# Stages behind the attention in tiles of 32 tokens of all batch rows, with the attention spread evenly over an LSTM's steps, in a one-core kernel

## The chip, the cores and the metric

The kernel runs on one core of a Trainium2 chip. The metric is the device time of one execution in microseconds, the median of the runs. The engines are PE (TensorE: matrix products and transposes), DVE (VectorE), ACT (ScalarE), POOL (GpSimd) and SP, which here only issues transfers. Each runs its own list of instructions in order and waits on semaphores for the others.

## What is computed

x is 4 x 512 x 256, fp32. First a transformer block in hyperbolic space is added to x, then an LSTM over the 512 tokens is added to that. `plin` is `expmap0(logmap0(x) @ w + b)`; the maps and mobius_add only need a row's norms and dot products as factors.

```python
q, k, v = _to_heads(plin(xm, w_q, b_q)), ...          # 16 heads of 16 columns
scores = einsum('bhqd,bhkd->bhqk', qt, kt) / sqrt(HD)
out_h = expmap0(einsum('bhqk,bhkd->bhqd', softmax(scores), vt))
x = mobius_add(residual, expmap0(g_msa * logmap0(plin(_from_heads(out_h), w_o, b_o))))
xm = expmap0(layer_norm(logmap0(x)) * (1 + sc_mlp) + sh_mlp)
ff = plin(plin(xm, w_f1, b_f1), w_f2, b_f2)           # 256 -> 1024 -> 256
block = mobius_add(x, expmap0(g_mlp * logmap0(ff)))
x = x_in + block
a = x[:, t] @ Wx + b + prev_h @ Wh                    # 512 steps, each needs the one before
i, f, o, g = sigmoid(a0), sigmoid(a1), sigmoid(a2), tanh(a3)
next_c = f * prev_c + i * g;  next_h = o * tanh(next_c)
return x + h
```

## The kernel before

The work comes in four stretches. **Setup** loads weights, gets the first layer norm's factors on POOL, and splits `Wh` into two fp16 words. The **loop over 16 tiles** of 128 tokens makes q, k and v, their heads' clips, and the split, transposed k (`norm_x`, L541 on PE; L1101 to L1139 on DVE; L805 to L813 on ACT; L401 to L406 on POOL). **Block 0**, the first 128 tokens of all four batch rows, then goes through attention and all stages behind it with no step beside it. After that come the **512 steps** of the LSTM in four blocks of 128. While block j - 1 is stepped through, `whole(j, step)` puts the attention and later stages of block j between the steps, in a run-time loop over j; the last block's steps have nothing beside them.

The order is written by hand. `along_attention` walks over 68 steps: behind each step every engine does its share of one head (`scores` L578 and `weighted` L591 on PE, `exps` L830 with two exponentials of 512 columns on ACT, `low_weights` L330 with 512 columns on DVE). Then `Slots` places the later stages between the remaining 60 steps: projection (L625), squares (L871, L873) and factors (`mobius` on POOL, ended by L432), sum and statistics (L1214, L1218), logarithm and norm (`to_norm`), the feed-forward per tile in six slots (L650, L646, L660), the second mobius_add and the gates' inputs from `Wx` (L682, copied by L937).

A step (`pe_step`, `act_step`, `dve_step`) is 32 products of 8 columns (L708) into banks for A, F and O; three sums on DVE (L1239, L1241, L1243), three tanh on ACT (L944 to L948), L1246 and a scan L1249 on DVE, tanh on ACT (L950), and then h in two fp16 words (L1257, L1258, L1260), on which the next step's products wait:

```python
d.tensor_tensor(hi, by_k(oU), by_k(tC), ALU.mult).then_inc(s["l_hi"], 1)
d.tensor_tensor(h32[:], oU[:], tC[:], ALU.mult).then_inc(s["l_h32"], 1)
v.wait_ge(s["l_h32"], m)
d.tensor_tensor(lo, by_k(h32), hi, ALU.subtract).then_inc(s["l_lo"], 1)
```

Behind it stand two copies nothing urgent waits for (L1261, L1263), then DVE's share of the other work. Every 16 steps `put_round` (L691) puts the gates' inputs into the banks. POOL makes its factors by chains of operations on 1 to 4 columns, each waiting for the one before (`power` is L226).

## Time and profile before

| | us |
|---|---|
| median of 3 runs | 1853.12 (1852.63 to 1854.8) |
| the profiled execution | 1852.16 |
| its span | 1850.4 |
| PE busy | 1204.1 (65%) |
| DVE busy | 1187.2 (64%) |
| ACT busy | 929.5 (50%) |
| POOL busy | 254.4 (14%) |
| mean granted TensorE clock | 0.627 |

No engine is busy all the time. The steps depend on one another, so that an engine's busy time matters only where its other work delays a step. PEclk is the share of full speed that TensorE was granted, 0.5 being 1.2 GHz and 1.0 being 2.4 GHz. PE counts an fp32 product as two instructions.

### The profile page before, as it was taken

Reading aid. Unit: us, or ns where it says so; the run is one execution under the profiler, and the core shown is the slowest. Engines: PE = TensorE matmul, PEld = TensorE weight load, DVE = VectorE, ACT = ScalarE, POOL = GpSimd, SP = SyncE. Lnnn points to the kernel's source line nnn. Section 1 sums busy time; section 2 is a strip of 40 time slices with the busy share of each in tenths; the row PEclk is TensorE's granted clock in tenths of the full one; section 3 lists DMA queues with packets and bytes.
Section 4 is the critical chain, followed back from the end, with each engine's and each line's share of the span. In section 5 each row is a group of like instructions: output and inputs, shape, how many; then the busy total and the mean of one; then the engine's idle time right before and its main releaser. Section 6 shows DMA issues by size and latency. Waiting matters only on the chain.

```text
span 1850.4 us, 59130 instructions
## 1 busy us (share of the span) xinstructions
PE 1204.1 (65%) x21615; PEld 988.4 (53%) x21615; DVE 1187.2 (64%) x6784; ACT 929.5 (50%) x3253; POOL 254.4 (14%) x674
## 2 busy tenths in 40 slices
PE   4666577186777648867776497777754885544444
PEld 4544455155666546666665366666653674444444
DVE  6466666222888766658887566588875755666665
ACT  0333378244777545547775455577753553333333
POOL 4222200522000031300001312000023220000000
PEclk9667655588555558965555598655555985555555
DMA  8000000000000000000000000000000000000000
GB/s 264 0 0 0 0 1 1 1 1 1 3 3 3 2 2 2 2 27 3 3 3 2 2 2 2 27 3 3 3 2 2 2 2 13 2 2 2 2 2 13
DMA packets 14654, 19.17 MB, mean 10 GB/s; under 512 B 3348, under 2 KB 13208, under 8 KB 14360
## 3 DMA queue, kind: packets, MB, share of 16 engines
q1 hardware_dynamic: 10248, 10.50, 1.8%
q10 hardware_dynamic: 4112, 4.86, 0.9%
q8 instruction: 172, 2.82, 0.6%
q14 instruction: 122, 1.00, 0.2%
HBM read 13.25 MB, written 2.10 MB: 8 GB/s over the span
## 4 chain that ended last, share of the span: by engine, by line
PE 42%; DVE 25%; ACT 12%; issue 11%; POOL 7%; DMA 1%; POOLq 1%; ACTq 1%; DVEq 0%; SPq 0%
PE psum L708 21%; DVE cnew L1249 4%; ACT tC L950 4%; DVE h L1257 3%; DVE h L1260 3%; PE psum L682 3%; DVE gO L1243 3%; PE psum L691 3%; POOL sc L226 3%; PE psum L650 3%; PE psum L660 2%; PE psum L541 2%; DVE cadd L1246 2%; DVE h L1258 2%; PE psum L578 2%
## 5 line engine op out<-in xcount | busy, mean ns | idle before, releaser
L708 PE MATMUL psum<-h,wh 128*128 128x8 f16 x16384 | 514.5, 168 | 419.5 <-DVE h L1260 402.5
L708 PEld LDWEIGHTS psum<-h,wh 128*128 128x128 f16 x16384 | 477.8, 103 | 533.2 <-DVE h L1260 501.8
L944 ACT ACTIVATE tA<-gA 128x16 f32<-128x16 f32 x512 | 110.5, 216 | 475.3 <-DVE gA L1239 475.1
L1239 DVE TENSOR_REDUCE gA<-psum 128x16 f32<-128x32 f32 x512 | 97.3, 190 | 180.1 <-PE psum L708 179.7
L578 PE MATMUL psum<-qT,kT 64*128 64x128 f16 x1024 | 153.8, 303 | 12.7 <-ACT weights L830 11.4
L950 ACT ACTIVATE tC<-cnew 128x8 f32<-128x8 f32 x512 | 108.8, 213 | 90.1 <-DVE cnew L1249 37.0
L830 ACT ACTIVATE weights<-psum 128x512 f16<-128x512 f32 x256 | 153.0, 598 | 0.0
L1257 DVE TENSOR_TENSOR h<-oU,tC 128x8 f16<-128x8 f32 x512 | 89.1, 174 | 94.7 <-ACT tC L950 94.1
L1249 DVE TENSOR_TENSOR_SCAN cnew<-cmul,cadd 128x24 f32<-128x24 f32 x512 | 107.7, 210 | 29.1 <-DVE cadd L1246 1.5
L1246 DVE SCALAR_TENSOR_TENSOR cadd<-tA 128x8 f32<-128x8 f32 x512 | 84.3, 165 | 52.4 <-ACT tA L944 44.6
L946 ACT ACTIVATE cmul<-gF 128x8 f32<-128x8 f32 x512 | 107.5, 210 | 0.0
L948 ACT ACTIVATE tO<-gO 128x8 f32<-128x8 f32 x512 | 105.6, 206 | 0.3
L591 PE MATMUL psum<-vs,weights 128*128 128x33 f16 x2048 | 101.7, 192 | 1.1 <-DVE weights L330 1.1
L578 PEld LDWEIGHTS psum<-qT,kT 64*128 64x128 f16 x1024 | 86.7, 127 | 26.0 <-ACT weights L830 11.4
L1260 DVE TENSOR_TENSOR h<-h 128x8 f16<-128x8 f32 x512 | 88.5, 173 | 18.1
L1243 DVE TENSOR_REDUCE gO<-psum 128x8 f32<-128x16 f32 x512 | 88.4, 173 | 16.1
L445 POOL TENSOR_SCALAR sc<-sc 128x64 f32<-128x64 f32 x4 | 1.9, 465 | 695.1 <-ACT sc L855 695.1
L330 DVE TENSOR_TENSOR weights<-tmp,weights 128x512 f16<-128x512 f32 x128 | 87.6, 684 | 13.7 <-ACT weights L830 13.7
L330 DVE TENSOR_TENSOR weights<-fT,weights 128x512 f16<-128x512 f32 x128 | 87.6, 684 | 11.3 <-ACT weights L830 11.3
L1241 DVE TENSOR_REDUCE gF<-psum 128x8 f32<-128x16 f32 x512 | 88.4, 173 | 8.4
L591 PEld LDWEIGHTS psum<-vs,weights 128*128 128x128 f16 x2048 | 80.3, 107 | 13.4 <-issue 10.6
L830 ACT ACTIVATE fT<-psum 128x512 f32<-128x512 f32 x128 | 76.2, 595 | 22.3 <-PE psum L591 21.8
(222 smaller groups left out, 2196.8 us busy)
## 6 DMA issues: line engine op xcount, KB each, us to landing
arena<-in_x_dram SPq DMA_DIRECT2D x4, 512.0 KB, 9.7
wf<-in_L_cond_w_f_dram SPq DMA_DIRECT2D x2, 1024.0 KB, 19.8
xs<-in_x_dram SPq DMA_DIRECT2D x4, 512.0 KB, 5.4
out_dram<-place SPq DMA_DIRECT2D x16, 128.0 KB, 1.7
arena<-in_L_cond_w_ada_dram ACTq DMA_DIRECT2D x1, 1536.0 KB
weights<-in_L_cond_Wh_dram ACTq DMA_DIRECT2D x1, 1024.0 KB, 14.3
gates<-in_L_cond_b_ada_dram ACTq DMA_DIRECT2D x8, 128.0 KB, 15.3
wx<-in_L_cond_Wx_dram SPq DMA_DIRECT2D x1, 1024.0 KB, 22.3
```

What stands on the lines that cost most here:

```text
L330: return engine.tensor_tensor(weights[:, buf, 1, kcs, :], w32[buf][:, half], weights[:, buf, 0, kcs, :], ALU.subtract)
L578: last = mm(bank[half][:, kc * P:(kc + 1) * P], tile_of(kT, b)[rows, hp, kc * P:(kc + 1) * P], qT[rows, hp, :], start=True, stop=True, ski ...
L591: last = mm(sums(h), weights[:, hp % 2, wl, 2 * e + kc // 2, kc % 2 * P:(kc % 2 + 1) * P], tile_of(vs, b)[:, kc, h, :], start=kc == 0 and ...
L708: last = mm(cols, wh16[:, half, kc, (g0 + g) * P:(g0 + g + 1) * P], h16[:, kc, :, :], start=False, stop=g == n - 1 and kc == KD - 1 and ha ...
L830: last = A(dst.rearrange("p a b -> p (a b)"), bank[half], ACT.Exp, scale=1.0 / (math.sqrt(HD) * QK_UP * QK_UP))
L944: A(tA[:], gA[:], ACT.Tanh, scale=down).then_inc(s["l_tA"], 1)
L950: A(tC[:], cnew[:, :, 2], ACT.Tanh, scale=0.5).then_inc(s["l_tC"], 1)
L1243: d.tensor_reduce(gO[:], gate_cols(pO, 2, r), axis=AX.X, op=ALU.add).then_inc(s["l_gO"], 1)
L1246: d.scalar_tensor_tensor(cadd[:, :, 2], tA[:, 0:8], 1.0, tA[:, 8:16], ALU.add, ALU.mult).then_inc(s["l_ig"], 1)
L1249: d.tensor_tensor_scan(cnew[:].rearrange("p c e -> p (c e)"), cmul[:].rearrange("p c e -> p (c e)"), cadd[:].rearrange("p c e -> p (c e)") ...
L1257: d.tensor_tensor(hi, by_k(oU), by_k(tC), ALU.mult).then_inc(s["l_hi"], 1)
L1260: d.tensor_tensor(lo, by_k(h32), hi, ALU.subtract).then_inc(s["l_lo"], 1)
```

## The change

- **The names.** A *slot* `t` runs from -192 to 511 on every engine (`for t in range(FIRST, T)`). From slot 0 on, each slot begins with recurrence step `t`; behind it `pieces` places the slot's share of the attention, of `merged` (the 16 heads of one tile brought together), of `post` (all stages behind the attention) and of the output. Nothing is a loop at run time any more: all 704 slots are written out, on every engine.
- **Attention.** One head takes two slots instead of one: its scores and its first exponential (fp32) in the even slot, its second exponential (fp16) in the odd one, its low words on DVE in two halves of 256 columns, its product with the values five slots after its scores. 96 of the 256 heads come before step 0, the other 160 ride along with steps 0 to 319.
- **Tiles behind the attention.** A tile is 32 tokens of each of the 4 batch rows (128 rows), so that one tile feeds 32 steps; before, it was 128 tokens of one batch row, and four of them fed 128 steps. `post(n, r)` runs tile n through r = 0 to 47, from slot 32n - 48; two tiles overlap in each 16 slots. Tile 0 is done wholly before step 0, and tile 1 to r = 15. `merged(k, r)` stands 32 slots apart, r = 0 to 8.
- **Transposed q.** q is split and transposed in the loop over the 16 tiles (`qstack`, `p_hq`, `p_qT`) and copied by ACT to `qTs`, behind the copy of k; before, this was done tile by tile in the attention (`q_twice`, `q_transposed`, `q_columns`).
- **Factors.** mobius_add's factors, the clips and the norm's factor are made on POOL for one tile (width 1) instead of four or two. The logarithm is no longer ACT's `Ln`: it is an estimate from the float's bits (DVE copy, POOL scale) with one correction by `Exp`, so that the table of functions is never changed in the slots. The gates' rows are multiplied by DVE instead of POOL (L437).
- **Feed-forward.** The first product is made transposed (16 products of 128 columns with `wf1` as the stationary side), ACT adds the bias column while copying, so that the 8 transposes and both DVE passes over 512 columns go; the norm of the hidden row is now the product of the squares `fsq` with a column of ones, 8 products with one column each.
- **Step.** The low half of h comes from a scan over 24 columns that multiplies and subtracts at once, in place of the product h32 and a subtraction; h for the output is a product of its own, behind it. `put_round`, the fp32 products that put 16 steps' gates into PSUM, stands ahead of its step instead of right behind the step before.
- **Transfers.** x comes in and the output leaves in pieces of 32 rows, four DMAs a tile, 16 tiles.

The core of the diff, with the pieces that the prediction speaks of:

```diff
+FIRST = -192
+PAUSE = 48
+HEADS = B * NB * H
+RING = 32
 ROUND = 16
...
+def head_slot(n):
+    return FIRST + 2 * n
...
+def merged_slot(k):
+    return head_slot(H * k + H - 1) + 6
...
+def pieces(g, attention, merged, post, out):
+    attention(g)
+    k = (g - merged_slot(0)) // RING
+    if 0 <= k < NT:
+        merged(k, g - merged_slot(k))
+    newest = (g + PAUSE) // RING
+    for n in (newest - 1, newest):
+        if 0 <= n < NT and g + PAUSE - RING * n < PAUSE:
+            post(n, g + PAUSE - RING * n)
+    if g > RING and g % RING == 1:
+        out(g // RING - 1)
...
+            def post(n, r):
...
+                if r == 1:
+                    hold(pool, "n_n1", n + 1)
+                    hold(pool, "n_n2", n + 1)
+                    mobius_arg(ch, "A", "n_ar")
+                if r == 4:
+                    hold(pool, "n_xa", n + 1)
+                    hold(pool, "n_xq", n + 1)
+                    hold(pool, "n_th", n + 1)
+                    mobius_factors(ch, "A", one("xq"), "n_ab")
+                if r == 8:
+                    hold(pool, "n_st", n + 1)
+                    to_ratio(ch, 1, mv1[:, 0:1], mv1[:, 1:2], one("x2q"), s["n_z"])
+                if r == 10:
...
+                if r == 12:
...
+                    to_norm(ch, 1, mv1[:, 0:1], mv1[:, 1:2], one("kapn"), one("negm"), s["n_km"], km_out_scaled=False)
+                if r == 21:
+                    hold(pool, "n_nu", n + 1)
+                    clip(ch, one("sun"), one("nun"), 1, one("cau"), one("cbu"), s["n_su"])
+                if r == 31:
+                    hold(pool, "n_nfc", n + 1)
+                    clip(ch, one("sfn"), one("nfn"), 1, one("caf"), one("cbf"), s["n_sf"])
+                if r == 34:
+                    hold(pool, "n_n3", n + 1)
+                    mobius_arg(ch, "B", "n_ar2")
+                if r == 37:
+                    hold(pool, "n_xa2", n + 1)
+                    hold(pool, "n_th2", n + 1)
+                    mobius_factors(ch, "B", one("x2q"), "n_ab2")
...
+            for t in range(FIRST, T):
+                pieces(t, lambda t: None, merged, post, lambda n: None)
...
+            def attention(t):
+                if t % 2 == 1 and 0 <= (t - 5 - FIRST) // 2 < HEADS:
+                    weighted((t - 5 - FIRST) // 2)
+                if t % 2 == 0 and (t - FIRST) // 2 < HEADS:
+                    scores((t - FIRST) // 2)
...
+                if 25 <= r < 29:
+                    i = r - 25
+                    pe.wait_ge(s["n_uc"], n + 1)
+                    if i > 0:
+                        pe.wait_ge(s["n_fc"], 4 * n + i)
+                    for c in (2 * i, 2 * i + 1):
+                        for kc in range(KD):
+                            last = mm(pP[:, c % 4 * P:(c % 4 + 1) * P], wf1[:, kc, c * P:(c + 1) * P], uT[:, 0, kc, :],
+                                      start=kc == 0, stop=kc == KD - 1, skip_group_check=True)
+                    last.then_inc(s["n_f"], 1)
+                if 29 <= r < 33:
+                    i = r - 29
+                    if i == 0:
+                        pe.wait_ge(s["n_fc"], 4 * n + 4)
+                    for kc in (2 * i, 2 * i + 1):
+                        last = mm(pP[:, 0:D], fT[:, kc, :], wf2[:, kc, :], start=kc == 0, stop=kc == KF - 1, skip_group_check=True)
+                    if i == 3:
+                        last.then_inc(s["n_f2"], 1)
+                if r in (30, 31):
+                    if r == 30:
...
+                    for c in range(4 * (r - 30), 4 * (r - 30) + 4):
+                        last = mm(pM[:, 0:1], fsq[:, c, :], ones[:, 0:1], start=c == 0, stop=c == KF - 1, skip_group_check=True)
+                    if r == 31:
+                        last.then_inc(s["n_nf"], 1)
...
+                if 42 <= r < 46:
+                    i = r - 42
...
+                    for gi in (2 * i, 2 * i + 1):
+                        c = CHUNK[gi]
+                        for kc in range(KD):
+                            last = mm(pP[:, gi % 4 * P:(gi % 4 + 1) * P], wx[:, kc, c * P:(c + 1) * P], XT[:, kc, :],
+                                      start=kc == 0, stop=kc == KD - 1, skip_group_check=True)
+                    last.then_inc(s["n_g"], 1)
...
+            def low_weights(m, half):
+                part = slice(half * T // 2, (half + 1) * T // 2)
+                v.wait_ge(s["t_e"], m + 1)
+                d.tensor_tensor(weights[:, m % 2, 1, part], w32[:, m % 2, part], weights[:, m % 2, 0, part], ALU.subtract).then_inc(s["t_l"], 1)
...
-                hi, lo = (h16[:, :, :, half] for half in range(2))
-                by_k = lambda t: t[:].rearrange("p (k b) -> p k b", b=B)
-                d.tensor_tensor(hi, by_k(oU), by_k(tC), ALU.mult).then_inc(s["l_hi"], 1)
-                d.tensor_tensor(h32[:], oU[:], tC[:], ALU.mult).then_inc(s["l_h32"], 1)
-                v.wait_ge(s["l_h32"], m)
-                d.tensor_tensor(lo, by_k(h32), hi, ALU.subtract).then_inc(s["l_lo"], 1)
+                by_k = lambda t: t.rearrange("p (k b) -> p k b", b=B)
+                d.tensor_tensor(hcol, by_k(oU), by_k(tC), ALU.mult).then_inc(s["l_hi"], 1)
+                v.wait_ge(s["l_hi"], m)
+                d.tensor_tensor_scan(lo3, ot3[:].rearrange("p c e -> p (c e)"), hi3, 0.0, ALU.mult, ALU.subtract).then_inc(s["l_lo"], 1)
```

How the order moves, on PE where the feed-forward stands between the steps. `wf`, `fT` and `arena` are the feed-forward's weights and hidden rows (`arena` holds `fT` and `fsq` in the changed kernel), `h` and `hl` are the LSTM's state. Before, in a row:

```order
L708 MATMUL psum<-h,wh 128x8 x32
L643 REGISTER_ALU
L646 MATMUL psum<-ident,tmp 128x128 x4
L650 MATMUL psum<-wf,uT 128x512
L702 REGISTER_ALU
L708 MATMUL psum<-h,wh 128x8 x32
L660 MATMUL psum<-wf,fT 128x256 x3
L631 MATMUL psum<-ident,xn 128x128 x2
L702 REGISTER_ALU
L708 MATMUL psum<-h,wh 128x8 x32
L646 MATMUL psum<-ident,tmp 128x128 x4
L660 MATMUL psum<-wf,fT 128x256
```

After, from the slot with r = 30 on, into the slot with r = 32, which is also r = 0 of the next tile:

```order
L562 MATMUL psum<-qTs,kT 128x128 x4
L634 MATMUL psum<-wf,arena 128x256 x2
L647 MATMUL psum<-ones,arena 128x1 x4
L687 MATMUL psum<-hl,wh 128x8 x32
L574 MATMUL psum<-vs,weights 128x33 x8
L634 MATMUL psum<-wf,arena 128x256 x2
L647 MATMUL psum<-ones,arena 128x1 x4
L677 MATMUL psum<-arena,ident 128x256
L677 MATMUL psum<-arena,ident 128x128 x2
L687 MATMUL psum<-hl,wh 128x8 x32
L562 MATMUL psum<-qTs,kT 128x128 x4
L634 MATMUL psum<-wf,arena 128x256 x2
```

Each step's 32 products are followed by a head's scores (L562) or its product with the values (L574), and then by the products behind the attention, and in front of every sixteenth step stand the three of L677.

On DVE, behind the last small operation of a step, where a tile's statistics are made. Before:

```order
L1214 SCALAR_TENSOR_TENSOR place<-place,sc 128x256
L1218 BN_STATS mv<-place 128x6
L1220 BN_AGGR mv<-mv 128x2
L1238 REGISTER_ALU
L1239 TENSOR_REDUCE gA<-psum 128x16
```

After, at the slot where r = 40 of one tile meets r = 8 of the next (`X` is the rows of the residual, `weights` the attention's low words):

```order
L1032 TENSOR_TENSOR weights<-w,weights 128x256
L1123 SCALAR_TENSOR_TENSOR X<-X,sc,xr 128x256
L1125 SCALAR_TENSOR_TENSOR X<-place,sc,X 128x256
L1093 BN_STATS mv<-X 128x6
L1095 BN_AGGR mv<-mv 128x2
L1131 TENSOR_REDUCE gA<-psum 128x16
```

Three long operations more stand between a step's end and the next step's sum L1131: half a head's low words, and the two of the older tile's second mobius_add.

## Rows read from the trace of the kernel before

**Rows 1.** Stretches: length, busy us and count of each engine, PEclk, DMA share, GB/s.
```profile
242.00:324.60 82.60, 63.35 (x808) 44.55 (x808) 52.91 (x106) 74.13 (x142) 0.00 (x0) 0.51 0.01 1
324.60:452.90 128.30, 67.44 (x318) 48.35 (x319) 25.75 (x66) 47.72 (x128) 46.19 (x133) 0.78 0.00 1
452.90:816.60 363.70, 262.04 (x5266) 217.73 (x5265) 257.29 (x1583) 212.12 (x779) 45.87 (x133) 0.63 0.02 4
1539.30:1850.40 311.10, 144.38 (x4146) 132.06 (x4146) 193.72 (x1412) 106.19 (x512) 0.00 (x0) 0.50 0.02 5
```

**Rows 2.** Timeline of one plain step, last block: start, us, engine, line, operation.
```profile
1560.92 1.02 PE L708 MATMUL psum<-h,wh 128*128 128x8 f16 x32 [1.34 <-DVE h L1260]
1561.55 0.19 DVE L1239 TENSOR_REDUCE gA<-psum 128x16 f32<-128x32 f32 x1 [0.53 <-PE psum L708]
...
1562.77 0.17 DVE L1257 TENSOR_TENSOR h<-oU,tC 128x8 f16<-128x8 f32 x1 [0.17 <-ACT tC L950]
...
1563.05 0.17 DVE L1260 TENSOR_TENSOR h<-h 128x8 f16<-128x8 f32 x1
...
1563.28 1.01 PE L708 MATMUL psum<-h,wh 128*128 128x8 f16 x32 [1.34 <-DVE h L1260]
```

**Rows 3.** Timeline of a step that carries attention.
```profile
1304.86 0.68 DVE L330 TENSOR_TENSOR weights<-fT,weights 128x512 f16<-128x512 f32 x1
...
1305.72 0.39 PE L591 MATMUL psum<-vs,weights 128*128 128x33 f16 x8
...
1306.04 0.60 PE L578 MATMUL psum<-qT,kT 64*128 64x128 f16 x4
...
1307.52 0.60 ACT L830 ACTIVATE weights<-psum 128x512 f16<-128x512 f32 x1
```

**Rows 4.** The chain of waits where one block ends and the next begins.
```profile
812.23 4.60 issue
```

**Rows 5.** Timeline of the loop over 16 tiles: POOL, DVE, ACT.
```profile
132.22 0.57 POOL L226 TENSOR_TENSOR sc<-sc,cst 128x1 f32<-128x1 f32 x1 [0.18 <-POOL sc L274]
...
133.44 0.73 DVE L1132 CAST qhl<-place 128x256 f32 x1 [0.21 <-DVE place L1124]
134.10 0.28 DVE L1133 CAST words<-place 128x256 f16<-128x256 f32 x1
...
137.29 1.02 ACT L813 ACTIVATE kT<-psum 128x1024 f16 x1 [6.53 <-PE psum L560]
```

**Rows 6.** POOL in its chains: a power 16 columns wide; a product 4 wide.
```profile
22.13 2.94 POOL sc L226
...
347.45 0.20 POOL L432 TENSOR_TENSOR sc<-sc 128x4 f32<-128x4 f32 x1 [0.18 <-POOL sc L431]
```

**Rows 7.** Timeline, DVE work between two steps, behind the attention.
```profile
669.79 0.48 DVE L1214 SCALAR_TENSOR_TENSOR place<-place,sc 128x256 f32<-128x256 f32 x1
670.30 0.43 DVE L1218 BATCH_NORM_STATS2 mv<-place 128x6 f32<-128x256 f32 x1
670.88 0.18 DVE L1220 BATCH_NORM_AGGREGATE mv<-mv 128x2 f32<-128x6 f32 x1 [0.15 <-DVE mv L1218]
```

**Rows 8.** Timeline of TensorE: fp32 products at either clock.
```profile
699.54 0.99 PE L639 MATMUL psum<-ones,usq 128*128 128x1 f32 x4
...
708.91 1.14 PE L691 MATMUL psum<-arena,ident 128*128 x6
709.89 1.46 PE L660 MATMUL psum<-wf,fT 128*128 128x256 f32 x6
...
769.68 3.54 PE L682 MATMUL psum<-uT,wx 128*128 128x128 f32 x16
...
778.27 2.05 PE L682 MATMUL psum<-uT,wx 128*128 128x128 f32 x16 [1.07 <-ACT uT L928]
```

**Rows 9.** A stretch of feed-forward work between steps; columns as in rows 1.
```profile
710.00:750.00 40.00, 37.70 (x617) 28.40 (x615) 29.05 (x185) 23.43 (x97) 10.42 (x31) 1.00 0.01 2
```

**Rows 10.** Timeline of ACT: four copies of the gates' inputs.
```profile
773.38 1.63 ACT L937 ACTIVATE arena<-psum,blc,unit 128x128 f32 x4 [0.96 <-PE psum L682]
```

More of the change, by code:

```diff
@@ L752, in _ @@
[L752 to L762 removed]
+                last.then_inc(s["t_AV"], 1)
+            def attention(t):
[3 more added lines that the diff above has]
+                    scores((t - FIRST) // 2)
@@ new lines, in gate_products @@
+            def gate_products(which, r):
+                bk, g0, w = GATE_BANKS[which]
+                for c in range(w):
+                    cols = gate_cols(which, r)[:, c * B:(c + 1) * B, :]
+                    for kc in range(KD):
+                        for half in range(2):
+                            last = mm(cols, wh16[:, half, kc, (g0 + c) * P:(g0 + c + 1) * P], hl[:, :, kc, :, 2].rearrange("p e b -> p b e"),
+                                      start=False, stop=c == w - 1 and kc == KD - 1 and half == 1, skip_group_check=True)
+                return last
@@ L764, in _ @@
+            for t in range(FIRST, T):
+                if t >= 0:
+                    step(t)
+                pieces(t, attention, merged, post, out_rows)
+            out_rows(NT - 1)
         @block.scalar
@@ L801, in _ @@
             act.sem_inc(s["p_kc"], 1)
+            act.sem_inc(s["p_qc"], 1)
             norm_x(0, 0, True)
@@ L943, in act_step, with step @@
+            def step(i):
+                m = i + 1
                 act.wait_ge(s["l_gA"], m)
@@ L1012, in _ @@
-            whole(0, None)
-            down = nc.scalar.alloc_register("down")
-            nc.scalar.reg_load(down, big1[0:1, 0:1].bitcast(I32))
-            with act.Fori(1, NB) as j:
-                whole(j, act_step)
-            for i in range(P):
-                act_step((NB - 1) * P + 1 + i, None, i % ROUND)
+                A(tC, cnew[:, :, 2], ACT.Tanh, scale=0.5).then_inc(s["l_tC"], 1)
+            for t in range(FIRST, T):
+                if t >= 0:
+                    step(t)
+                pieces(t, attention, merged, post, lambda n: None)
@@ L1341 @@
+            for t in range(FIRST, T):
+                if t == 0:
+                    v.wait_ge(s["n_xc"], 4)
+                    v.wait_ge(s["h0_s"], 1)
+                    d.tensor_tensor(xw[:, 0], xw[:, 0], h0c[:], ALU.add).then_inc(s["l_x0"], 1)
+                if t >= 0:
+                    step(t)
+                pieces(t, attention, merged, post, out_rows)
+            out_rows(NT - 1)
 _INS = ["x", "cond_1024"] + [f"L0_cond_{n}" for n in ("w_q", "b_q", "w_k", "b_k", "w_v", "b_v", "w_o", "b_o", "w_f1", "b_f1",
```

1104 lines of the change are left out of this document (437 added, 667 removed).

## The prediction

> **What bounds the kernel now.** I read the stretches first, then single steps in the timeline, then the chain of waits at one boundary. The stretches [rows 1] give four parts: up to 242.0 us setup and the loop over 16 tiles; to 324.6 the attention of block 0, where ACT is busy 74.13 of 82.6 us; to 452.9 the later stages of block 0, where no engine is busy for more than half and the chain between engines sets the time; then the 512 steps. The last block has nothing beside its steps: 311.1 us, of which some 5.7 lie behind its last step, so a plain step takes 2.36 us [rows 2], 2.355 over the block. Inside it PE is busy 1.02 us and idle 1.34, and DVE has about 0.68 us between its last small copy and the next sum L1239, which starts 0.63 us after PE. The first 384 steps take 1539.3 - 452.9 = 1086.4 us, 182 more than 384 plain steps (904). With the last block's 4 that is **186 us that other work adds to the steps**. The attention itself adds next to nothing: the step of [rows 3] has one head's two exponentials on ACT (0.60 each), 0.68 us of DVE and 0.39 + 0.60 us of PE, and it is as long as a plain one. So the price of work between steps is what overflows an engine's gap, and of the 186 us most stands in the 60 steps a block that carry the later stages. Some is neither: at a block's end the chain shows 4.60 us of "issue" [rows 4], in which PE waits for nothing but its instructions.
>
> **The change, up to step 0.** The loop over tiles gets a second ACT copy of 1024 columns behind that of k. The one of k takes 1.02 us [rows 5] and ACT's square of the next tile waits behind it, so each of 16 rounds grows by up to 1.02 us. DVE's cast of q took 0.73 us where the cast of k took 0.28 [rows 5]. If the run-time address is what made it slow, the written-out target gives back 0.45. If it is POOL, which works in the same moment, nothing comes back. I take 0.8 a round from the two ends 0.57 and 1.02: **+13 us** (9 to 16), so 255, and 256 at the first exponential.
> The Trainium skill (SBUF — State Buffer, "SBUF: two separate sides") says that VectorE and GpSimd share one pair of ports, which one of them holds for a whole instruction. By that rule the loop would pay the 16 us.
>
> Then 72 of the 96 heads run alone, at two exponentials or 1.2 us a head [rows 1, 3]: 86 us. In them four tiles are merged. DVE waits at r = 7 for POOL's chain that began at r = 2: some 12 operations of 0.20 + 0.18 us idle [rows 6], and a power 16 columns wide, 2.94 us [rows 6], in all 8 us, where five slots of 0.6 us give 3. ACT runs one slot ahead and loses 4 us, and 0.8 for its two extra copies: 4 x 5 = 20 us. That is 362. Tile 0 now goes alone from r = 0 to 47: POOL's chains (two of 7, two of 13, one of 10, one of 29 operations and two clips, 10 of them powers at 0.57 + 0.18 [rows 5]) are 39 us; PE, ACT and DVE in between, by their rows, 40 us. Tile 1's first 16 slots push two of POOL's chains in front of tile 0's, +10, and 24 heads share the slots, +8: 97 us. Block 0's four tiles took 128.3 us for the same [rows 1]. **Step 0 starts at 459 us instead of 452.9: +6.** Ends: 435 (all waits for POOL hidden) to 485.
>
> **The step.** Today L1257 starts at 1562.77 and L1260 at 1563.05, and PE 0.23 later [rows 2]. The new low half waits for the high half's end (0.17 + 0.04) and is a scan of 24 columns, which in this kernel (L1249) takes 0.04 more than L1260. 0.21 + 0.04 against 0.28: 0.025 us less a step, **-13 us** over 512. Ends: 0 and -20.
>
> **Other work between the steps.** An excess is what an engine's share adds beyond its gap. With attention, the gaps left are about 0.7 (even slots) or 0.9 us (odd) on PE, 0.35 on DVE (half a head's low words take some 0.33 of 0.68) and 0.9 on ACT; without it 1.34, 0.68 and 1.4. One tile's 32 slots, with attention:
> - DVE: an operation of 256 columns is 0.48 [rows 7], a dependent second one 0.05 later. r = 20 (two, and a sum of heads in the same slot): 1.0. r = 33 with the next tile's r = 1 (three): 1.1. r = 40 with r = 8 (two, then statistics, 0.43 and 0.18 with 0.15 idle [rows 7]): 1.3. Three single ones: 0.4.
> - POOL: r = 4 of the new tile stands in front of r = 37 of the old one on its queue. 13 operations take 5.5 us each, so DVE at r = 40 is 1.1 us early: 1.1.
> - PE with ACT, feed-forward one (r = 24 to 28): each slot 4 fp32 products of 128 columns, 8 of which took 3.54 us at 1.2 GHz and 2.05 at 2.4 [rows 8]. Two slots still at 1.2 GHz: 0.85 and 1.05. Then two at 2.4 where ACT ends last, one with the squares, one with the merged tile's copy: 0.9 and 0.85. Transposes: 0.1.
> - PE, feed-forward two (r = 29 to 32): 256 columns at 0.5 us a product, one column at 0.25, half of the 0.99 for two at 1.2 GHz [rows 8]. r = 29: 0.15. r = 30, scores 0.6 + 1.0 + 1.1: 1.4. r = 31: 1.2. r = 32 with r = 0 and `put_round` (1.14 [rows 8]): 2.9. The period's other `put_round`: 0.8.
> - Gates (r = 42 to 45): 4 products, then two ACT copies of 0.4 us [rows 10]: 1.2, 0.6, 0.4, 0.2.
>
> Sum 17.5 us. 10 tiles lie beside attention: 175. Five lie beside steps alone; with the wider gaps the same list gives, in its order, 0.3, 0.8 and 1.0 on DVE, 1.1 for POOL, 1.2 and 3.9 for the two feed-forwards, 0.4 for the other `put_round`, 1.2 for the gates: 9.9, or 50 in all. The last period: 1. **226 us instead of 186: +40.** It replaces the block boundaries [rows 4] and ACT's table changes, which 186 contains and 226 doesn't. Everything is written out; the last block was too and ran at 2.355, so that costs nothing. Row transfers lie on SP, three tiles ahead: nothing. Behind the last step one tile instead of four: **-1**.
>
> Here the clock is weighed. Attention alone ran at 0.51 and plain steps at 0.50 [rows 1], but the dense feed-forward of block 1 at 1.00 with PE busy 37.70 of 40 us [rows 9]. The spread work is nearly gapless on PE from r = 25 to 32 and again at r = 42, so I take two slots at 1.2 GHz in each and 2.4 behind them.
> The Trainium skill (TensorE: Matmul & The Clock Gate, The HAM clock gate) says that the slow clock is the default and sustained activity lifts it. By that rule work spread thinly pays the slow price; it is the third rival.
>
> The sum: +6 - 13 + 40 - 1 = +32 on the profiled execution's 1852.2 us, which lies 1 us under the median: **1884 us**.
>
> **Rivals.** (1) *The clock stays up*, so the spread work fits. If PE keeps 2.4 GHz through r = 24 to 47, the slots at 1.2 GHz lose 2.9 us a tile and the scores 1.0: 10 x 3.9 + 5 x 2.0 = 49, **1835 us**, faster. It decides from 32 us on, or 2.1 a tile. For it: 1.00 in [rows 9], in which the steps' own narrow products were a third of PE's time. Against: the attention slots, busier than plain ones, ran at 0.51. (2) *The waits for POOL are hidden*: step 0 at 435 (-24) and no wait at r = 40 (-17): **1843 us**. For it: ACT and PE have slack there. Against: each engine's order is fixed. (3) *The clock never rises*: the same products at the slow prices of [rows 8] add 9.0 us a tile with attention and 7.5 without: +127, **2011 us**. For it: rows 1's 0.63 mean and the gaps of r = 33 to 41. Against: [rows 9].
>
> **How the numbers follow.** The forecast has 0.45, rival 1 0.27, rival 2 0.13, rival 3 0.15. The forecast's own range is 1860 to 1930, from the ends of the start and 3 us a tile. The whole range, 1815 to 1960, takes in rivals 1 and 2 and leaves out most of 3. A difference under 0.2% (3.7 us) can't be told from none here. Faster: rivals 1 and 2 nearly whole, 0.38; same 0.05; slower 0.57.
>
> **What would show it.** First product of a step at 459 us. 2.33 us for a plain step. Periods of 32 steps some 92 us long beside attention and 85 without. PEclk above 0.9 only in r = 27 to 33. Waits of DVE on POOL at r = 40. The prediction is wrong if periods beside attention take under 88 us, or if the clock is at one level throughout.

## The result: 5% slower, and the profile after

The changed kernel takes **1955.4 us** (median of 4 runs, 1936.2 to 1981.3) against 1853.0 for the one before: ratio 1.051, 95% interval 1.046 to 1.057. The forecast was 1884, so slower was right and the size was not: +102 us instead of +32. The profiled execution took 1959.4 us, of which 1957.6 are its span. The run of 1981.3 us counts as slow, because it lies over 1.5% above the fastest, and is left out of the ratio; four later runs of the same kernel, none of them slow, took 1949 to 1972 us.

The four runs alone already say where to look. They took 1936.2, 1951.3, 1959.4 and 1981.3 us, at a mean granted clock of 0.569, 0.560, 0.555 and 0.542, while the kernel before repeats within 2.2 us, at 0.627 in its profile. From the page of the changed kernel: the span, the busy times, TensorE's share and clock in the 40 slices.

```profile
span 1957.6 us, 60062 instructions
PE 1378.3 (70%) x22071; PEld 1183.1 (60%) x22071; DVE 1170.0 (60%) x6481; ACT 914.1 (47%) x3335; POOL 553.8 (28%) x1726
PE   3665666556787878787878787878776757675764
PEclk9767655565656555555555555555555555555555
```

From the 12th slice on the granted clock stands near 0.5 (a digit 5 is 0.50 to 0.59), that is at 1.2 GHz nearly throughout. The stretches, in the columns of [rows 1]: attention alone, tile 0 on its own, ten periods of 32 steps beside attention.

```profile
255.90:365.90 110.00, 67.81 (x852) 47.13 (x852) 60.62 (x170) 75.05 (x152) 27.73 (x52) 0.50 0.01 1
365.90:462.26 96.36, 48.70 (x405) 37.71 (x405) 26.92 (x82) 39.13 (x97) 42.19 (x141) 0.59 0.01 2
462.26:1422.85 960.59, 755.63 (x13411) 658.73 (x13409) 634.41 (x3767) 515.94 (x1994) 308.72 (x1002) 0.53 0.02 5
```

TensorE's products other than the steps' own, in the view of groups by line and shape: total busy time and the mean of one instruction in ns (an fp32 product is two instructions).

```profile
L663 PE MATMUL psum<-place,wx 128*128 128x128 f32 x512 | 130.4, 436 | 6.9 <-ACT arena L870 6.4
L626 PE MATMUL psum<-uT,wf 128*128 128x128 f32 x512 | 127.5, 429 | 1.1 <-ACT arena L845 0.8 <-ACT uT L838 0.2
L634 PE MATMUL psum<-wf,arena 128*128 128x256 f32 x256 | 114.6, 593 | 0.5 <-ACT arena L845 0.5
L647 PE MATMUL psum<-ones,arena 128*128 128x1 f32 x256 | 47.2, 305 | 0.0
```

The same work in the kernel before:

```profile
L682 PE MATMUL psum<-uT,wx 128*128 128x128 f32 x512 | 76.0, 312 | 10.7 <-ACT uT L928 10.7
L650 PE MATMUL psum<-wf,uT 128*128 128x512 f32 x128 | 74.9, 698 | 0.0
L660 PE MATMUL psum<-wf,fT 128*128 128x256 f32 x256 | 65.7, 389 | 1.0 <-ACT fT L910 1.0
```

The first three groups went from 217 us to 373 us with no more arithmetic in them: before, they came in dense stretches that ran mostly at 2.4 GHz; now they mostly run at 1.2. The eight one-column products a tile, which sum the squares of the feed-forward's hidden layer, came with the change (L647, 256 instructions; before, L639 had 64 for another norm).

**A tile whose clock rises and one whose clock does not.** The order of instructions is the same in all periods beside attention, and yet they are 89.8 to 99.0 us long. In order of time: 90.9, 89.8, 96.0, 93.7, 99.0, 98.6, 98.5, 98.9, 98.6, 94.4; then without attention 92.5, 92.3, 92.2, 92.3, 87.4; then the last, 73.1. I call g the step's number within its period; r = g + 16 for the tile in its later stages. Three slots make 7.0 of the 8.8 us between the second and the seventh period, g = 14, 15 and 16 (r = 30 to 32): feed-forward two, the norm's products, `put_round`, the next tile's output projection. The rest is in g = 12 and 13 (1.05 and 0.65 us). Here they are on TensorE in the second period, from the timeline:

```profile
591.48 0.95 PE L647 MATMUL psum<-ones,arena 128*128 128x1 f32 x8
592.29 1.00 PE L687 MATMUL psum<-hl,wh 128*128 128x8 f16 x32
593.14 0.35 PE L574 MATMUL psum<-vs,weights 128*128 128x33 f16 x8
593.35 1.11 PE L634 MATMUL psum<-wf,arena 128*128 128x256 f32 x4
594.29 0.95 PE L647 MATMUL psum<-ones,arena 128*128 128x1 f32 x8
595.10 1.12 PE L677 MATMUL psum<-arena,ident 128*128 128x256 f32 x6
596.06 1.00 PE L687 MATMUL psum<-hl,wh 128*128 128x8 f16 x32
```

And in the seventh:

```profile
1071.54 1.71 PE L647 MATMUL psum<-ones,arena 128*128 128x1 f32 x8
1073.11 1.00 PE L687 MATMUL psum<-hl,wh 128*128 128x8 f16 x32
1073.96 0.39 PE L574 MATMUL psum<-vs,weights 128*128 128x33 f16 x8
1074.19 2.05 PE L634 MATMUL psum<-wf,arena 128*128 128x256 f32 x4
1076.03 1.71 PE L647 MATMUL psum<-ones,arena 128*128 128x1 f32 x8
1077.60 2.05 PE L677 MATMUL psum<-arena,ident 128*128 128x256 f32 x6
1079.45 1.05 PE L687 MATMUL psum<-hl,wh 128*128 128x8 f16 x32
```

In these rows TensorE has no gap in either period, so its work is the slot. Only the fp32 products change price: 0.95 or 1.71, 1.11 or 2.05, 1.12 or 2.05. The steps' own 32 narrow products take 1.00 to 1.05 us either way. The slots g = 14 to 16 are 3.16, 3.65 and 3.81 us long in the second period, and 4.90, 6.39 and 6.34 in the seventh. The stretches around these rows and the two whole periods:

```profile
555.22:645.00 89.78, 69.21 (x1338) 60.89 (x1338) 63.33 (x376) 51.41 (x200) 30.63 (x100) 0.61 0.02 5
1032.39:1130.94 98.55, 78.45 (x1338) 68.08 (x1338) 63.32 (x376) 51.52 (x200) 30.59 (x100) 0.50 0.02 5
...
590.80:601.40 10.60, 10.29 (x156) 8.96 (x155) 5.92 (x37) 4.34 (x17) 1.02 (x3) 1.00 0.01 2
1052.50:1086.70 34.20, 34.20 (x410) 29.74 (x407) 15.71 (x95) 14.43 (x54) 3.72 (x12) 0.50 0.01 2
```

The counts are equal (1338, 376, 200, 100). What differs is the clock of one stretch. In the seventh period TensorE is busy without a gap for 34.2 us and stays at 1.2 GHz. [Rows 9], from which I took that dense work has 2.4 GHz, did not carry over. Beside attention, the clock of a period rises in g = 11 to 13 or late in g = 16, and in no period of this profile in g = 14 or 15. Five of the ten (the fifth to the ninth) never get it. The third has it from g = 11 and loses it in g = 14, before most of the crowded work; the fourth and the tenth lose it in g = 15 and get it back for the end of g = 16.

**The wait at r = 40**, in VectorE's timeline:

```profile
1107.38 0.48 DVE L1123 SCALAR_TENSOR_TENSOR X<-X,sc,xr 128x256 f32<-128x256 f32 x1 [1.56 <-POOL sc L430]
```

VectorE stands 1.56 us, and the sums of the next step stand behind it. Over the run the view of waits has this one at 26.2 us in 15 times, the longest 4.2 us.

### The profile page after: what moved, and what is told of

Same layout as the page of the kernel before. It is cut to its first block, busy times and chain, and to the rows that moved or that the text cites. A ratio compares the mean times of both kernels' runs of the same rounds, so it can differ in the third digit from the quotient of the medians.

```text
span 1957.6 us, 60062 instructions
## 1 busy us (share of the span) xinstructions
PE 1378.3 (70%) x22071; PEld 1183.1 (60%) x22071; DVE 1170.0 (60%) x6481; ACT 914.1 (47%) x3335; POOL 553.8 (28%) x1726
## 3 DMA queue, kind: packets, MB, share of 16 engines
q10 hardware_dynamic: 3392, 3.81, 0.7%
## 4 chain that ended last, share of the span: by engine, by line
PE 46%; DVE 13%; POOL 11%; issue 8%; ACT 8%; POOLq 1%; DVEq 0%; ACTq 0%
PE psum L687 18%; PE psum L663 7%; PE psum L626 6%; PE psum L634 5%; POOL sc L231 4%; PE psum L677 3%; DVE cnew L1140 3%; ACT ot L885 2%; DVE hl L1149 2%; PE psum L647 2%; DVE hl L1147 2%; PE psum L562 2%; DVE gO L1135 2%; ACT w L783 1%; ACT weights L787 1%
## 5 line engine op out<-in xcount | busy, mean ns | idle before, releaser
L687 PE MATMUL psum<-hl,wh 128*128 128x8 f16 x16384 | 525.9, 172 | 347.0 <-DVE hl L1149 346.4
L687 PEld LDWEIGHTS psum<-hl,wh 128*128 128x128 f16 x16384 | 505.9, 104 | 427.8 <-DVE hl L1149 408.0
L1131 DVE TENSOR_REDUCE gA<-psum 128x16 f32<-128x32 f32 x512 | 96.8, 189 | 281.4 <-PE psum L687 276.6
L1032 DVE TENSOR_TENSOR weights<-w,weights 128x256 f16<-128x256 f32 x512 | 208.2, 419 | 39.8 <-ACT weights L787 38.8
L231 POOL TENSOR_TENSOR sc<-sc,cst 128x1 f32<-128x1 f32 (+1 forms) x260 | 201.1, 773 | 48.1 <-POOL sc L279 18.1
L562 PE MATMUL psum<-qTs,kT 64*128 64x128 f16 x1024 | 151.1, 299 | 6.4 <-ACT weights L787 4.5
L783 ACT ACTIVATE w<-psum 128x512 f32<-128x512 f32 x256 | 149.8, 585 | 7.9 <-DVE weights L1032 5.5
L663 PE MATMUL psum<-place,wx 128*128 128x128 f32 x512 | 130.4, 436 | 6.9 <-ACT arena L870 6.4
L574 PE MATMUL psum<-vs,weights 128*128 128x33 f16 x2048 | 100.9, 191 | 39.8 <-DVE weights L1032 22.9
L626 PE MATMUL psum<-uT,wf 128*128 128x128 f32 x512 | 127.5, 429 | 1.1 <-ACT arena L845 0.8
L663 PEld LDWEIGHTS psum<-place,wx 128*128 128x128 f32 x512 | 112.9, 325 | 13.8 <-issue 11.6
L574 PEld LDWEIGHTS psum<-vs,weights 128*128 128x128 f16 x2048 | 78.8, 106 | 61.4 <-DVE weights L1032 56.9
L634 PE MATMUL psum<-wf,arena 128*128 128x256 f32 x256 | 114.6, 593 | 0.5 <-ACT arena L845 0.5
L626 PEld LDWEIGHTS psum<-uT,wf 128*128 128x128 f32 x512 | 112.4, 323 | 3.9 <-issue 3.1
## 6 DMA issues: line engine op xcount, KB each, us to landing
oT<-in_L_cond_Wh_dram ACTq DMA_DIRECT2D x1, 1024.0 KB, 14.4
```

The source lines that it names most:

```text
L231: ch.link(nc.gpsimd.tensor_tensor(dst, src, cst[:, which, 0:w], ALU.pow))
L562: last = mm(bank[m % 2][:, kc * P:(kc + 1) * P], kT[part, b, hp, kc * P:(kc + 1) * P], qTs[part, k, hp, :], start=True, stop=True, skip_gr ...
L574: last = mm(pV[:, h % 8 * W1:(h % 8 + 1) * W1], weights[:, m % 2, wl, kc * P:(kc + 1) * P], vs[:, k % B, kc, h, :], start=kc == 0 and wl = ...
L626: last = mm(pP[:, c % 4 * P:(c % 4 + 1) * P], wf1[:, kc, c * P:(c + 1) * P], uT[:, 0, kc, :], start=kc == 0, stop=kc == KD - 1, skip_group ...
L634: last = mm(pP[:, 0:D], fT[:, kc, :], wf2[:, kc, :], start=kc == 0, stop=kc == KF - 1, skip_group_check=True)
L663: last = mm(pP[:, gi % 4 * P:(gi % 4 + 1) * P], wx[:, kc, c * P:(c + 1) * P], XT[:, kc, :], start=kc == 0, stop=kc == KD - 1, skip_group_c ...
```

## The experiments

Two questions. Is the crowded stretch paid for by TensorE's work at whatever clock it has (**crowded slots**), or does something in the changed instruction stream (narrow products instead of 512-column ones, one-column products, gaps) hold the clock down (**clock rivals**)? And is the wait for POOL worth its length?

**Width of the products.** The changed kernel with one product of 512 columns for the four of 128 in each feed-forward slot. It leaves out the sum over the two halves of the inputs.

```diff
-for c in (2 * i, 2 * i + 1):
-    for kc in range(KD):
-        last = mm(pP[:, c % 4 * P:(c % 4 + 1) * P], wf1[:, kc, c * P:(c + 1) * P], uT[:, 0, kc, :], ...)
+last = mm(pP[:, :], uT[:, 0, i % 2, :], wf1[:, i % 2, i // 2 * 512:(i // 2 + 1) * 512], ...)
```

> Leaves out the feed-forward's first product as it should be: in place of 4 fp32 products of 128 columns a slot (r = 25 to 28) stands one of 512 columns, the same number of columns, without the sum over both halves, so that its output is not the reference's. Everything behind it stays. Theory A (what keeps TensorE at 1.2 GHz in the changed kernel is that its dense slots are made of products of 128 and 8 columns): the granted clock rises to 1.00 from about r = 27 on in most periods, the slots r = 30 to 32, now 4.9, 6.4 and 6.35 us, fall to about 3.0, 3.8 and 3.8, and the whole falls by 10 x 9 + 5 x 4 us to about 1850. Theory B (the work is simply too much for one kernel's slots at any mix, the clock follows the short gaps before and behind): the clock stays at 0.50, r = 25 to 28 get 0.3 us shorter each at most, the whole stays above 1930.

Measured: 1962.7 us, clock 0.555: nothing came of it. The other way round, the kernel before with its wide products cut into pieces of 128 columns. Its text below says that the sums are the same. They are not, and the output is not the reference's; but TensorE gets the same columns, in four or two times as many products.

> The kernel before with each feed-forward product of 512 columns cut into four of 128 and each of 256 into two of 128; nothing else changes, the sums are the same. Theory A: the stretch 710 to 750 us no longer has a granted clock of 1.00 but mostly 0.50, and the three blocks get longer, each by 10 to 20 us, the whole at 1885 to 1910. Theory B: the clock stays near 1.00 there and the whole rises by at most 10 us for the extra weight loads.

Measured: 1858.2 us, ratio 1.003 (1.002 to 1.005), clock 0.625. Its dense stretch, with the columns of [rows 9]:

```profile
705.00:750.00 45.00, 42.79 (x772) 40.95 (x771) 31.91 (x201) 25.78 (x105) 9.05 (x27) 0.97 0.01 3
```

Cut products ran at 2.4 GHz in the kernel before, and with the first product widened the changed one stayed at its low clock. The width of the feed-forward's products is not the cause.

**Gaps between the steps.** Extra products behind each of the 14 light slots a period (g = 0 to 7, 19 to 24); nothing is left out. First two or three fp16 ones of 256 columns:

```diff
+if 0 <= t < 480 and t % RING in (0, 1, 2, 3, 4, 5, 6, 7, 19, 20, 21, 22, 23, 24):
+    for _ in range(2 if t % 2 == 0 else 3):
+        mm(pP[:, 0:256], ident16[:], wh16[:, 0, 0, 0:256], ...)
```

> The changed kernel with idle gaps of PE filled: in the slots r = 35 to 40 and r = 48 to 55 of a period (of 32) two (even) or three (odd) fp16 products of 256 columns into a bank nobody reads then. If columns streamed are what is missing in the light slots (theory A in its strong form), the clock is at 1.00 when the feed-forward begins, r = 25 to 32 shrink by 10 us a period, and the whole falls to about 1830 to 1850. If not, the clock stays at 0.50 and the light slots grow by 0 to 0.2 us each, the whole stays within 1940 to 1990.

Measured: 1960.0 us, clock 0.552. Then two fp32 ones of 128 columns in the same places (`mm(pP[:, 0:128], ident[:], wx[:, 0, 0:128], ...)`):

> The changed kernel with two extra fp32 products of 128 columns (onto a free PSUM bank) behind each of the light slots g = 0 to 7 and 19 to 24; nothing is left out. A slot has some 1 us in which TensorE is idle, and two such products take 0.9 us at 1.2 GHz by the row of L663 (439 ns per instruction, two a product), so the light slots should stay within 0.3 us of 2.33 us. Theory (idle gaps between the steps are what keeps the clock low, whichever type fills them): the granted clock of the light slots and of g = 9 to 17 rises, mean clock above 0.65, and the time falls toward 1840 to 1900 us. Rival (filling the gaps does not raise the clock, as the fp16 products did not): the clock stays at 0.55 and the time at 1955 to 2010 us, by what the fillers add to 14 slots a tile.

Measured: 1967.6 us, clock 0.553. The light slots grew by up to 0.2 us as allowed for, and the clock did not rise for it:

```profile
690.00:700.00 10.00, 10.00 (x143) 9.41 (x143) 5.73 (x36) 6.32 (x24) 0.00 (x0) 0.50 0.01 2
700.00:710.00 10.00, 10.00 (x102) 8.70 (x102) 3.99 (x24) 3.11 (x11) 0.00 (x0) 0.50 0.01 2
...
sum 200.00, PE 185.05 PEld 162.97 DVE 129.01 ACT 104.75 POOL 61.41; mean PE 9.25 PEld 8.15 DVE 6.45 ACT 5.24 POOL 3.07
```

TensorE was busy 185 of 200 us (620 to 820), at 1.2 GHz in every 10 us of them. So filling the gaps did not bring the clock there; three of its later periods had 2.4 GHz in g = 14 and 15 all the same, where the unaltered kernel had two.

**The norm's products.** Seven of the eight left out (and with them most of the norm's sum):

```diff
-for c in range(4 * (r - 30), 4 * (r - 30) + 4):
-    last = mm(pM[:, 0:1], fsq[:, c, :], ones[:, 0:1], start=c == 0, stop=c == KF - 1, ...)
+if r == 31:
+    last = mm(pM[:, 0:1], fsq[:, 0, :], ones[:, 0:1], start=True, stop=True, ...)
```

> Leaves out 7 of the 8 products that sum the squares of the hidden row (the norm comes from one eighth of the row, so that the output is not the reference's). If r = 30 and 31 are bound by PE at 1.2 GHz, each loses 3 to 4 products of 0.5 us (r = 30: 2.0 us, r = 31: 1.5 us), 3.5 us a period with 15 periods, about 50 us: 1900. If ACT, DVE or POOL ended those slots, the time would hardly change (above 1940).

Measured: 1886.4 us, 69 less, clock 0.575. The products alone explain 48 of it at the slow price (7/8 of 2 x 1.71 us in 16 tiles), and less where the clock had risen; the rest is the clock. Next a version that computes all, with the squares and the ones in bf16:

```diff
-fsq = arena[:, 3072:4096].rearrange("p (c t) -> p c t", c=KF)
+fsq = arena[:, 3072:3584].bitcast(BF16).rearrange("p (c t) -> p c t", c=KF)
...
-last = mm(pM[:, 0:1], fsq[:, c, :], ones[:, 0:1], ...)
+last = mm(pM[:, 0:1], fsq[:, c, :], ones16[:, 0:1], ...)
```

> The squares of FF1's output are written in bf16 and summed by products in bf16 instead of fp32; the eight products stay where they are and everything is computed. In the changed kernel's cold tile L647 took 16 x 0.334 us by the profile's sum of 3.4 us less overlaps, and leaving seven of the eight out gave 69 us back. Crowded slots (TensorE sets the length of the slots r = 30 and 31, at either clock): a bf16 product of one column should take what the narrow fp16 ones take, near 0.17 to 0.19 us each, so 8 x 0.43 - 8 x 0.18 = 2.0 us a tile less, 16 tiles, 32 us: about 1923 us, and slots g14 and g15 fall from 4.9 and 6.4 to near 3.9 and 5.4 us. Rival (the narrow fp32 products are what holds the clock down in the crowded stretch): the clock stands at 2.4 GHz in those slots in most tiles and the time falls to 1880 or below. Rival (products of one column are bound by their weight load whatever the type): no change, 1955.

Measured: **1888.8 us** (1876 to 1900), ratio to before 1.016 (1.013 to 1.020): 67 less, twice the forecast.

```profile
L649 PE MATMUL psum<-ones,arena 128*128 128x1 bf16 x128 | 8.6, 171 | 0.0
```

The 47.2 us of L647 became 8.6. The crowded slots of a period at 1.2 GHz (the one from 1014.4), on TensorE:

```profile
1054.80 2.06 PE L636 MATMUL psum<-wf,arena 128*128 128x256 f32 x4
1056.64 0.29 PE L649 MATMUL psum<-ones,arena 128*128 128x1 bf16 x4
1056.80 2.05 PE L679 MATMUL psum<-arena,ident 128*128 128x256 f32 x6
```

Four products take 0.29 us where they took 1.71, and slots g14 and g15 are 3.48 and 4.97 us instead of 4.90 and 6.39: 2.8 us a tile, of which I had expected 2.0. With 0.4 in g16, in which the clock now rises near the end, such a period is 95.3 us long instead of 98.5. Over sixteen tiles that is some 50 us. The rest of the 67 is the clock: of the ten periods beside attention only three are that long, and two are at 88.4 and 88.9. Slot g = 16 had its short length of 3.81 us in seven of the ten, where the changed kernel had it in two. In g = 14 and 15 the gain is not clear: three of ten against two. The clock rival doesn't hold in its clean form: were the one-column fp32 products what holds the clock down, all tiles would have the high one now. Whether the shorter stretch or the missing fp32 products brought the clock to g = 16 is not separated by this run.

**The wait for POOL.** VectorE's two instructions at r = 40, and the transposes and gate products behind them, one slot later (in the diff VectorE's block first, then that of TensorE, which ScalarE's follows).

```diff
-if r == 40:
+if r == 41:
     v.wait_ge(s["n_ab2"], n + 1)
...
-if r == 41:
+if r == 42:
...
-if 42 <= r < 46:
+if 43 <= r < 47:
```

> The two VectorE instructions of r = 40 (L1123, L1125) stand one slot later, and the transposes and gate products behind them one slot later too; nothing else changes. Theory: VectorE waited there 1.56 us for POOL's last factor (L430 of the changed kernel), and the recurrence of step 25 stood behind it; one slot later the factor is there. Expected: slot g24 falls from 5.08 to about 3.5 us, 16 tiles x 1.56 = 25 us less, about 1930 us. Rival (POOL or the gates are late next, so the wait only moves, to the first put_round behind the gates): slots g31 and g0 grow by what g24 loses, 1955 us.

Measured: **1907.8 us** (1905 to 1921), 48 less. In VectorE's timeline the instructions no longer wait:

```profile
1096.55 0.48 DVE L1123 SCALAR_TENSOR_TENSOR X<-X,sc,xr 128x256 f32<-128x256 f32 x1
1097.07 0.48 DVE L1125 SCALAR_TENSOR_TENSOR X<-place,sc,X 128x256 f32<-128x256 f32 x1
```

Slot g24 fell from 5.08 to 2.50 us, by more than the wait: the statistics of the next tile (r = 8) stand there alone now. Summed over the run, the slots g = 4, 17 and 24 lost 36 us, the gate slots and g = 31 grew by 10, and g = 13 to 16 lost 28: as in the last experiment, fewer periods were long there. Nothing in those slots was changed, so what stands elsewhere in a period bears on the clock that its crowded slots meet. All four runs (1905 to 1921) lie below all eight of the unaltered kernel (1936 to 1981).

**Both together.**

> norm16 and late40 together. They touch different slots, so their gains should add: 1955 - 32 - 25 = 1898 us. If it is far below the sum of the two, the clock has risen in more tiles; if above, one gain hid in the other.

Measured: **1846.8 us** (10 runs, 1845.6 to 1854.8), 109 less than the change and below the kernel before: ratio 0.997 (0.996 to 0.999). The measured gains add (67 + 48 = 115), but the forecast of 1898 was 51 us too high, and by its own words that means that the clock has risen in more tiles. So it has: g = 14 and 15 stood at 2.4 GHz in eight of the ten periods beside attention, g = 16 in all ten, and those periods are 86.1 to 88.9 us long. The ten runs are 9 us apart, and those of the unaltered kernel 36 us (1936 to 1972).

**One more product out of the crowded slots:** on top of both, the bias of the output projection (L611, 555 ns an instruction) as two bf16 products.

```diff
-mm(pM[:, 0:D], ones[0:1, :], bo[0:1, :], start=False, stop=True, ...).then_inc(s["n_wo"], 1)
+for half in range(2):
+    last = mm(pM[:, 0:D], ones16[0:1, :], bo16[0:1, half, :], start=False, stop=half == 1, ...)
+last.then_inc(s["n_wo"], 1)
```

> The version with the bf16 norm sums and the later second residual, and besides the output projection's bias added by two bf16 products (high and low part of the bias) in place of one fp32 product, in slot g16. In the changed kernel L611 took 2 x 0.71 us by the profile's rows, 1.2 us of TensorE at 1.2 GHz; two bf16 products of 256 columns should take some 2 x 0.25 us. Crowded slots: slot g16 falls by 0.7 us where TensorE is at 1.2 GHz there and by 0.35 us where it is at 2.4 GHz, 15 tiles, so 1847 - 5 to 10 = 1837 to 1842 us. Rival (VectorE and ScalarE end that slot): no change, 1847.

Measured: **1842.7 us** (6 runs), ratio to before 0.9945 (0.9932 to 0.9958), the fastest of all: 0.3% under the last one by the two ratios, at the upper end of the forecast.

```profile
L615 PE MATMUL psum<-bo,ones 1*128 1x256 bf16 x32 | 6.4, 281 | 0.0
```

It took 0.3 us from slot g16 (3.81 to 3.52), in which TensorE had the higher clock in all periods beside attention, here as in the version before it.

**Does the instruction stream decide?** The changed kernel a second time, unaltered:

> The changed kernel itself, unaltered, for a second profile. Theory (whether the clock rises in the crowded slots of a tile is not decided by the instruction stream): other tiles than in the first profile show the long slots g14 to g16 (4.9, 6.4, 6.3 us), periods again lie between 90 and 99 us, and time and mean clock move together as in the first four runs (1936 us at 0.569 to 1981 at 0.542). Rival (the stream decides): the same tiles, 65 to 96 and 129 to 288, are the long ones, and the profiled time is within 3 us of 1959.

Measured: 1964.3 us (1949 to 1972). Periods of the profiled execution (1972.5 us): 98.5, 98.5, 98.5, 93.7, 98.9, 98.5, 98.5, 98.8, 98.5, 94.3, 87.0, 91.9, 92.0, 92.1, 87.4. The first and second periods, which ran at 2.4 GHz in their crowded slots in the first profile, did not in this one. The eleventh did, and only in this one. The rows are those of the second and the eleventh:

```profile
564.10:662.60 98.50, 78.44 (x1338) 68.03 (x1338) 63.23 (x376) 51.51 (x200) 30.60 (x100) 0.50 0.02 5
...
1442.43:1529.38 86.95, 60.23 (x1162) 54.70 (x1162) 53.20 (x344) 36.25 (x167) 29.29 (x99) 0.56 0.02 6
```

Last, the same with 30 wide fp32 products once ahead of step 0:

```diff
+if t == 0:
+    pe.wait_ge(s["n_xc"], 4)
+    for _ in range(30):
+        mm(pP[:, 0:D], ident[:], wx[:, 0, 0:D], ...)
```

> The changed kernel with 30 extra fp32 products of 256 columns once, ahead of step 0: by the row of L634 (593 to 672 ns per instruction, two a product) some 37 us of TensorE at 1.2 GHz, or 18 if the clock rises within them. Nothing else changes. Both theories: the clock goes to 2.4 GHz somewhere in this stretch of pure wide products if density alone decides (then about 25 us); it stays at 1.2 GHz (37 us) if it does not. Behind it the same 511 steps; if the tile's place in time decides the clock of the crowded slots, other tiles than before are the long ones, and the time is 1955 + 25 to 37 with a spread of 25 us around it; if the stream decides, exactly the delay is added.

Measured: 1953.4 and 1971.4 us. Step 0 came 18 us later, and the clock rose within the products:

```profile
460.00:470.00 10.00, 9.00 (x45) 7.30 (x42) 0.95 (x3) 3.21 (x8) 5.13 (x21) 0.55 0.00 0
470.00:480.00 10.00, 10.00 (x48) 8.81 (x47) 0.00 (x0) 0.00 (x0) 2.01 (x9) 1.00 0.01 2
```

Behind them other periods were the long ones: 93.6, 98.5, 98.5, 98.5, 94.1, and then 89.7, 91.0, 89.9, 91.0, 90.5, where the unaltered kernel has 98 to 99, and 94 in the tenth. So the 18 us more left the time where it was. Whether a tile meets the high clock is not decided by its instruction stream alone: the two profiles of the unaltered kernel show it. That the shift brought the other pattern is not shown, since the pattern also changed without it. That less work in and around the crowded slots meets the high clock more often is clearest in the version with both changes: eight of its ten periods had it in g = 14 and 15, against two and one in the profiles of the unaltered kernel and five in this one. What exactly decides stays open.

## Why the prediction was right in direction and wrong in size

Its steps in order, with the other work between the steps as the excess of each slot over 2.33 us, added up over all periods of the first profile. 511 steps at 2.33 are 1190.6 us; the trace has 1488.4 from the first step's last instruction (464.35) to the last step's (1952.73), so 297.7 us of other work.

| term | predicted | measured |
|---|---|---|
| first exponential / first output projection | 256 / 362 | 255.9 / 365.9 |
| tile 0 on its own | 97 | 96.4 |
| first product of a step | 459 | 462.3 |
| plain step | 2.33 | 2.33 |
| beside attention: VectorE and POOL slots (r = 20, 33, 40) | 49 | 45.6 |
| feed-forward one (r = 25 to 28) | 37.5 | 34.3 |
| **feed-forward two, norm, `put_round` (r = 29 to 32)** | 56.5 | **87.0** |
| **gates** | 24 | **37.7** |
| other `put_round`, rest | 8 | 8.3 |
| without attention: VectorE and POOL | 16 | 13.2 |
| feed-forward one | 6 | 10.2 |
| **feed-forward two, norm, `put_round`** | 19.5 | **43.6** |
| **gates** | 6 | **14.4** |
| rest, last period | 3 | 3.4 |
| sum of the other work | 226 | 297.7 |

The spans differ by 107.2 us. Of these 9.4 are the start (+6 forecast), -12.8 the step (-13), 111.7 the other work (297.7 for 186; +40 forecast), and -1 the end (-1). So 72 of the 75 us between 1884 and the profiled 1959.4 are other work, and the four bold rows alone are 77 over; the remaining rows are 5 under.

The steps themselves, the start within 3 us, and the structure of a period were right: the scan of 24 columns took the place of the last product ([rows 2]) as costed (0.28 less 0.25 is 0.03, where the prediction writes 0.025; measured were 2.355 to 2.33), and plain steps follow each other at 2.33 us:

```profile
1931.52 0.17 DVE L1147 TENSOR_TENSOR hl<-ot 128x8 f16<-128x8 f32 x1 [0.18 <-ACT ot L885]
1931.73 0.21 DVE L1149 TENSOR_TENSOR_SCAN hl<-ot,hl 128x24 f16<-128x24 f32 x1
...
1934.06 0.21 DVE L1149 TENSOR_TENSOR_SCAN hl<-ot,hl 128x24 f16<-128x24 f32 x1
```

The start was forecast from two ends, because VectorE's slow cast of q could be due to its run-time address or to POOL. The trace decides it. The cast of q, now to a written-out place, is short. The cast of k, which starts while POOL's product runs, is now the slow one (0.28 before, [rows 5]):

```profile
137.45 0.29 DVE L1009 CAST qstack<-place 128x256 f16<-128x256 f32 x1
137.54 0.68 POOL L375 TENSOR_TENSOR osq<-place,sc 128x256 f32<-128x256 f32 x1
137.66 0.71 DVE L1010 CAST stack<-place 128x256 f16<-128x256 f32 x1
```

So the slow cast goes with POOL's work and nothing came back. The first exponential came at 255.9 us, 13.9 behind 242.0; the two ends were 9 and 16.

**The step that failed** is "so I take two slots at 1.2 GHz in each and 2.4 behind them". The crowded slots r = 29 to 32 were priced at 2.4 GHz, 5.65 us a tile. In the two periods that had 2.4 GHz in all of them they cost less than that, 3.6 us (0 + 0.83 + 1.32 + 1.48 in the second one). In the five where it never rose they cost 11.3 us, in the third 10.4, in the fourth and tenth 6.4 and 6.5, or 8.7 on average. The gate slots never had it. Four fp32 products of 128 columns took 2.07 us at 1.2 GHz and 1.06 at 2.4 in the feed-forward of the second period (L626 at 579.5 and 585.8 us), and the four of a gate slot cost the former, here in the seventh period:

```profile
1111.97 2.07 PE L663 MATMUL psum<-place,wx 128*128 128x128 f32 x8
```

The gates cost 3.8 us a tile instead of 2.4. Had all periods been as the lucky ones (two at 90.4 beside attention, one at 87.0 without, in the second profile; 74.6 is a plain period), the other work would have been 10 x 15.8 + 5 x 12.4 + 1 = 221 us, against my 226. So the list was about right and its clock was wrong. That 221 comes so near to 226 is partly luck: in those periods the crowded slots cost 3.6 us for my 5.65, the gates 3.8 for my 2.4, and a period without attention 12.4 for my 9.9. The direction did not hang on the clock: 221 is still 35 more than the 186 of the kernel before, or some 30 with the start, the step and the end.

The third rival (the clock never rises, 2011 us, chance 0.15) had the mechanism, priced too high with attention: 26.5 us a tile for a period at 1.2 GHz, where 24.0 were measured; without attention its 17.4 meets the measured 17.7, though there the end of g = 16 had 2.4 GHz. The truth lies between forecast and rival 3, a little nearer to the rival (71 and 56 us off), and differs from run to run, which I had in no case. Of what should show it, "periods of some 92" came as 90 to 99, and the 85 without attention came as 92.3. "PEclk above 0.9 only in r = 27 to 33" held for where it rose, but in half of the periods beside attention it was above 0.9 nowhere.

Behind the row stood the Trainium skill (TensorE: Matmul & The Clock Gate, The HAM clock gate): the slow clock is the default, and sustained activity lifts it. It says as well that the chip's activity window runs freely, so that the same kernel has a cold start of different length from run to run. The runs show a variation of that kind, but in the middle of the kernel (the second period, 89.8 us in one profile and 98.5 in the other); that it comes from the window is not shown. With the first part the trace agrees only partly: TensorE was busy 100% of 690 to 710 us with the fillers, and 34.2 of 34.2 us at 1052.5 to 1086.7 here, both at 1.2 GHz. The page calls the effect small for a typical kernel; here the runs of one kernel lie between 1936 and 1972 us, 1.9% apart.

The POOL wait was the right place and too small (1.1 forecast, 1.56 measured); VectorE's own work in these slots was less than forecast, so that both together came to 45.6 for 49. Rival 1 (clock stays up) is refuted by the profile; rival 2 (POOL's waits hidden) by the 462.3 us of step 0 and the wait at r = 40.

## What to carry to other kernels

When work that ran in dense blocks is spread over a recurrence, price TensorE's fp32 products at 1.2 GHz first, and the other clock only as what may be given back. Then look at the few slots in which the engine has no gap: everything there costs its full length. The norm's sum in bf16 gave back 67 us where its own price was some 50, because the clock rose more often; the bias in bf16, in a slot that had the high clock already, gave back no more than its price. The 14 light slots a period took two more products for at most 0.2 us each. A wait on the recurrence's engine costs its length in every period; with its consumer one slot later, the slots concerned lost 36 us and those behind them grew by 10.
